# Three denominator terms for four in a masked attention kernel, with one PE step fewer and a finer wait for the mask

## The reference

```python
h = relu(layernorm(x))                       # x: 8 graphs x 1024 nodes x 512, fp32
q, k, v = heads(h @ Wq + bq), heads(h @ Wk + bk), heads(h @ Wv + bv)   # 16 heads of 32
scores = q k^T / sqrt(32);  scores = -inf where adj == 0               # adj: 8 x 1024 x 1024 int32
x + (softmax(scores) @ v) @ Wo + bo
```

## Time and profile before

| | us |
|---|---|
| median of 3 runs | 2085.54 (2085.31 to 2088.58) |
| the profiled execution | 2085.51 |
| its span, first to last instruction | 2083.6 |
| PE busy (matmul) | 1932.5 |
| DVE busy | 1557.3 |
| ACT busy | 1478.1 |
| POOL busy | 1302.1 |

### The profile page before, as it was taken

One profiled execution on the slowest core, in us unless ns is written; L12 is line 12 of the kernel. 1 busy time (PEld: TensorE's weight loads), 2 busy tenths in 40 slices (PEclk: granted clock), 3 DMA queues, 4 the chain that ended last, 5 costly groups with the idle time before them and its releaser, 6 DMA issues.

```text
span 2083.6 us, 40441 instructions
## 1 busy us (share of the span) xinstructions
PE 1932.5 (93%) x14336; PEld 776.5 (37%) x14336; DVE 1557.3 (75%) x1587; ACT 1478.1 (71%) x1765; POOL 1302.1 (62%) x581
## 2 busy tenths in 40 slices
PE   3799899998999999999999999999899998999977
PEld 2334344343344333443334333334333343444312
DVE  5688777878768787687867877778767787767773
ACT  3577786677867788668876778767777677866672
POOL 0377567556666567656667557666557566676574
PEclk8999999999999999999999999999999999999999
DMA  5433244342444324343351434424234332442302
GB/s 177 122 87 96 82 112 132 88 107 64 120 112 124 83 76 132 86 122 86 92 142 56 115 93 117 119 74 119 81 109 122 88 106 66 117 122 64 74 1 81
DMA packets 103222, 206.61 MB, mean 99 GB/s; under 512 B 11616, under 2 KB 11744, under 8 KB 103008
## 3 DMA queue, kind: packets, MB, share of 16 engines
q1 hardware_dynamic: 103008, 203.80, 35.2%
HBM read 153.43 MB, written 50.33 MB: 98 GB/s over the span
## 4 chain that ended last, share of the span: by engine, by line
PE 76%; DVE 7%; issue 6%; DMA 5%; ACT 2%; POOL 1%; SPq 1%; DVEq 0%; ACTq 0%; POOLq 0%
PE ps L694 20%; PE ps L681 19%; PE ps L654 15%; PE ps L705 10%; PE ps L668 7%; PE ps L661 6%; DVE ring L905 4%; DMA k_stack<-k_parts 2%; DMA k_parts<-k_part 1%; SPq L513 1%; DMA edges<-adjT 1%; ACT hT_hi L776 1%; DVE k_part L918 1%; POOL acc L1079 1%; ACT ring L770 1%
## 5 line engine op out<-in xcount | busy, mean ns | idle before, releaser
L905 DVE TENSOR_TENSOR ring<-ps,mask 128x1024 f32<-128x1024 f32 x1024 | 1234.6, 1219 | 435.7 <-PE ps L681 399.9
L770 ACT ACTIVATE ring<-ring 128x1024 f32<-128x1024 f32 x1024 | 1069.7, 1051 | 382.9 <-DVE ring L905 374.6
L1079 POOL TENSOR_TENSOR acc<-ring 128x1024 f32<-128x1024 f32 x256 | 604.1, 2371 | 730.2 <-ACT ring L770 729.4
L681 PE MATMUL ps<-q_stack,k_stack 128*128 128x512 f16 x2048 | 610.4, 382 | 85.2 <-DVE ring L905 61.4
L1079 POOL TENSOR_TENSOR acc<-acc,ring 128x1024 f32<-128x1024 f32 x256 | 617.6, 2432 | 0.0
L694 PE MATMUL ps<-ring,v_sb 128*32 128x512 f32 x4096 | 509.1, 604 | 0.0
L681 PEld LDWEIGHTS ps<-q_stack,k_stack 128*128 128x128 f16 x2048 | 157.1, 98 | 481.8 <-DVE ring L905 246.4
L694 PEld LDWEIGHTS ps<-ring,v_sb 128*32 128x32 f32 x4096 | 100.9, 109 | 252.3 <-issue 218.1
L705 PE MATMUL ps<-acc,ones 128*32 128x512 f32 x1024 | 139.8, 597 | 2.7 <-issue 2.6
L705 PE MATMUL ps<-ring,ones 128*32 128x512 f32 x1024 | 137.3, 592 | 0.0
L661 PE MATMUL ps<-wv_hi,hT_hi 128*128 128x128 f16 x1024 | 103.1, 219 | 3.2 <-DVE k_part L918 3.2
(11 more groups left out here) (80 smaller groups left out, 1593.4 us busy)
## 6 DMA issues: line engine op xcount, KB each, us to landing
x_in<-x SPq DMA_DIRECT2D x168, 256.0 KB, 2.7
edges<-adjT SPq DMA_DIRECT2D x128, 256.0 KB, 2.9
q_stack<-q_parts SPq DMA_DIRECT2D x128, 256.0 KB, 4.9
k_stack<-k_parts SPq DMA_DIRECT2D x128, 256.0 KB, 5.0
q_parts<-q_part SPq DMA_DIRECT2D x32, 512.0 KB, 2.7
k_parts<-k_part SPq DMA_DIRECT2D x32, 512.0 KB, 2.9
out<-x_in SPq DMA_DIRECT2D x56, 256.0 KB, 2.1
ring<-x SPq DMA_DIRECT2D x2, 1024.0 KB, 6.6
```

The lines of the kernel that those rows point to most:

```text
L681: i = nc.tensor.matmul(ps_s(j)[:, hh, :], stack["k"][:, up % 2, h, kt * P:(kt + 1) * P], stack["q"][:, up % 2, h, half * HALF:(half + 1) * ...
L770: nc.scalar.activation(tile, tile, ACT.Exp, scale=SCALE / UP / UP).then_inc(s["prob_ready"], 1)
L905: nc.vector.tensor_tensor(ring[:, slot_of(kt, pair), :].rearrange("p (a n) -> p a n", n=HALF), ps_s(j), mask[:, kt:kt + 1, half * HALF:(ha ...
L1079: nc.gpsimd.tensor_tensor(acc[:, group, pair, :], first_of, ring[:, slot_of(kt, pair), :], ALU.add).then_inc(s["sum_done"], 1)
```

## The change

- A denominator has three terms. A is the sum of key tiles 0 to 3, B of 4 to 6, key tile 7 is read from `ring`. POOL makes 5 x 2 adds a sweep.
- The blocks of a sweep stand in four steps, 6, 10, 14 and 18; those of step 16 move to 18, and A goes from 10 to 14. Step 16 becomes a slot for pieces of chunks.
- DVE's waits for a free slot of `ring` are written anew for this: for the weighted sum of the key tile that was in it, and for the add that read it, or for the last term.
- DVE waits for the mask by key tile, ahead of every second tile, and no longer for eight pieces ahead of a sweep.
- The mask pieces stand behind other tiles of the fourth and the first unit.

```diff
-BLOCKS = {6: ("p0", "p1"), 10: ("p2", "p3", "dA"), 14: ("p4", "p5"), 16: ("p6", "dB", "d6"), 18: ("p7", "d7")}
-TERMS = "AB67"
+BLOCKS = {6: ("p0", "p1"), 10: ("p2", "p3"), 14: ("p4", "p5", "dA"), 18: ("p6", "dB", "p7", "d7")}
+TERMS = "AB7"
+
+SUMMED = {1: 0, 2: 2, 3: 4, 5: 6, 6: 8}
+SUMS = 10
+SUMMED_AT = {"A": 6, "B": 10}
...
-MASK_AT = {3: [17, 18, 20, 22, 24, 26, 28, 30], 0: [1, 3, 5, 7, 8, 9, 11, 13]}
+MASK_AT = {3: [17, 19, 21, 23, 25, 27, 29, 30], 0: [3, 5, 8, 11, 13, 16, 19, 22]}
...
-                    pe.wait_ge(s["sum_done"], 8 * V + 4 * (TERMS.index(term) + 1))
+                    pe.wait_ge(s["sum_done"], SUMS * V + SUMMED_AT[term])
...
-                if kt < RING_KT:
-                    if not very_first:
-                        if kt < 2:
-                            dve.wait_ge(s["pv_done"], 8 * V + kt - 3)
-                            dve.wait_ge(s["sum_done"], 8 * V + 2 * kt - 3 + pair)
-                        else:
-                            dve.wait_ge(s["den_done"], len(TERMS) * V + kt - 3)
-                else:
-                    dve.wait_ge(s["pv_done"], 8 * V + kt - 3)
-                    dve.wait_ge(s["sum_done"], 8 * V + {4: 1, 5: 1, 6: 3, 7: 5}[kt] + pair)
+                before = (V - 1, kt + QT - RING_KT) if kt < RING_KT else (V, kt - RING_KT)
+                if not (kt < RING_KT and very_first):
+                    W, k = before
+                    dve.wait_ge(s["pv_done"], QT * W + k + 1)
+                    if k == QT - 1:
+                        dve.wait_ge(s["den_done"], len(TERMS) * (W + 1))
+                    else:
+                        dve.wait_ge(s["sum_done"], SUMS * W + SUMMED[k if k in SUMMED else k + 1] + pair + 1)
...
-                        if up == 0 and j % SWEEP == 0:
-                            dve.wait_ge(s["mask_ready"], b * 2 * QT + QT * (j // SWEEP + 1))
+                        if up == 0 and j % PAIRS == 0:
+                            dve.wait_ge(s["mask_ready"], b * 2 * QT + j // PAIRS + 1)
...
-                group, k = divmod(kt, 3)
+                group, n = kt // 4, SUMS * V + SUMMED[kt] + pair
                 pool.wait_ge(s["prob_ready"], U * TILES + j + 1)
-                if k == 1 and pair == 0 and not very_first:
+                begins = kt % 4 == 1
+                if begins and pair == 0 and not very_first:
                     pool.wait_ge(s["den_done"], len(TERMS) * (V - 1) + group + 1)
-                if k == 2:
-                    pool.wait_ge(s["sum_done"], 8 * V + 4 * group + pair + 1)
-                first_of = ring[:, slot_of(kt - 1, pair), :] if k == 1 else acc[:, group, pair, :]
+                if not begins:
+                    pool.wait_ge(s["sum_done"], n - 1)
+                first_of = ring[:, slot_of(kt - 1, pair), :] if begins else acc[:, group, pair, :]
...
-                        if j % SWEEP // PAIRS in (1, 2, 4, 5):
+                        if j % SWEEP // PAIRS in SUMMED:
```

## The result

| | before | after |
|---|---|---|
| median of 4 runs, us | 2086.53 (2085.31 to 2088.58) | 2062.02 (2058.85 to 2063.42) |
| ratio, 95% interval | | 0.988 (0.986 to 0.990) |
| the profiled execution, us | 2085.51 | 2058.85, span 2057.1 |
| granted clock over the span | 0.989 | 0.980 |

The change made the kernel 1.2% faster. 2044.1 was forecast, so 18 us of the expected gain are missing, 15 by the profiled execution. The time lies inside the range, near its slow end: the forecast's own bounds ended at 2062, and only rival (b), which did not happen, took the range to 2067. Most of what the forecast says of the sum is in the trace, and the loss is in the one part that it priced at nothing.

What follows compares the result with a forecast made beforehand. TensorE's (PE's) own work was taken as the bound in most of the kernel. The terms -69.1 + 27.0 + 6.0 + 4 - 4.1 - 3.2 - 5.0 + 3 = -41.4 us gave 2044.1 us, range 2021 to 2067.

Steps and rivals of the forecast that it cites:

- rival (b): GpSimd's loop is 1 to 2 us a sweep longer than summed, so sweeps wait: 2064 to 2079 us; chance 0.11.
- Part 1, the term less: In each of 64 sweeps, one denominator block less takes 1.08 us off PE: -69.1 us.
- Part 2, the hole: Two scores-only steps at a unit's end leave PE idle 1.04 us at 26 ends: +27.0 us (15 to 45).
- rival (a): The new idle time at ends of units doesn't appear: 2017 us; chance 0.08.
- Part 3, GpSimd: GpSimd's 128 more adds keep up in every sweep except in the last unit: +6.0 us.
- the loop's 26.4 us: GpSimd's cycle of adds, term B and reciprocal takes 26.4 us, longer than the last sweep's 22.6: +3.8 us there.
- (c): GpSimd's loop sets every sweep, making the kernel slower: 2108 us; chance 0.05.
- Port contention: VectorE's `oT_lo` gets half an add longer beside GpSimd in 24 of 32 cases: +4 us on PE (0 to 12).
- Part 4, mask pieces and the finer wait: Moving mask pieces and waiting by key tile on VectorE costs and gains nothing: 0 us (-3 to +5).
- Part 5: Projection pieces shift as step 16 becomes a slot: -4.1, -3.2, -5.0 and +3 us in the first three units.
- the third unit's k: Its second half starts in the same step in which its bank is freed: +3 us (0 to 6).

Runs made afterwards that it cites:

- p6_step16: The changed kernel with the weighted sum of key tile 6 moved back to step 16, still a slot for chunk pieces; 2054.0 us.
- last_pieces: The changed kernel with mask pieces 2 to 5 of the fourth unit moved back to their old tiles; 2035.1 us.
- mask_before: The changed kernel with all mask pieces and VectorE's coarse mask wait as before the change; 2038.2 us.
- stack_first: The changed kernel with the load of `k_stack` issued one tile earlier in the fourth unit; 2061.0 us.
- store_first: The changed kernel with both the store of `k_parts` and the load of `k_stack` one tile earlier in the fourth unit; 2035.7 us.
- pool_plus: unit3_pieces with one or two more GpSimd adds of 1.28 us in every sweep, results unused; 2047.2 and 2079.3 us.
- unit3_pieces: The changed kernel with the fourth unit's mask pieces at their tiles of before; 2033.3 us.
- mask_alone: The kernel before the change with only the new mask pieces and the new finer wait; 2096.5 us, ratio 1.005.

## Why the prediction was right or wrong

**Part 1, the term less: right.** -69.1 us was forecast on PE, and its own work between the scores fell by 68.2. The extrapolated step of four blocks takes 4.10 us (4.12).

**Part 2, the hole: right.** 1.05 us at each of the 24 ends of units inside the graphs (1.04), and 0.98 in the row of a graph end outside the loop. That is some 27 us, and rival (a) is out. p6_step16 takes the hole away at the cost that its own row shows.

**Part 3, GpSimd: right in the body, short at the end.** Term B follows GpSimd's last add at once in the last three sweeps and in one of the first graph, in no other. There the last sweep was to take the loop's 26.4 us and takes 28.7, from the reciprocal at 1992.29 to that at 2021.00. PE's timeline of after shows it:

```profile
2010.13 1.04 PE L698 MATMUL ps<-ring,v_sb 128*32 128x512 f32 x8
2015.58 1.93 PE L709 MATMUL ps<-acc,ones 128*32 128x512 f32 x8 [4.41 <-POOL acc L1082]
2017.29 1.93 PE L698 MATMUL ps<-ring,v_sb 128*32 128x512 f32 x8
2019.00 1.93 PE L709 MATMUL ps<-ring,ones 128*32 128x512 f32 x8
```

PE waits 4.41 us, and what follows runs at half clock: a block each 1.71 us and not 0.86, three times, 2.6 us that no row could show, since PE did not wait there. So the loop of 26.4 us was right in size, and the term lacked the clock. The output projection starts at half clock too, for 5.1 us (2025.53 to 2030.63), where before it was 2.8. In all, the last unit and what is behind its last scores cost 11.7 us more than before (3.5 lost in the unit, 8.2 behind it), where 6.0 stood in the sum; in last_pieces, mask_before, stack_first and store_first, with the same last unit, it is 9. Rivals (b) and (c) are out as the kernel stands, and the two pool_plus runs confirm how close they are.

**Port contention: too high, from a wrong reading.** `oT_lo` was to cost PE 4 us. Its group in after:

```profile
L962 DVE SCALAR_TENSOR_TENSOR oT_lo<-o_raw,b_up,oT_hi x32: 1274/1364/3350, 136.0 to 2024.2; 128x1024 f16<-128x1024 f32 x32
```

Minimum, median and maximum stand as in the earlier trace rows (1273, 1341, 3482). The mean rose from 1816 to 1843 ns, 0.9 us over all 32. The step that failed is "The median of 1.34 says that most run undisturbed now", and with it that these would get half an add longer. In before, 24 of the 32 already met a GpSimd instruction; in after 31 do. Two of them in after, VectorE's row and the rows of GpSimd beside it:

```profile
990.63 1.34 DVE L962 SCALAR_TENSOR_TENSOR oT_lo<-o_raw,b_up,oT_hi 128x1024 f16<-128x1024 f32 x1
990.84 3.36 POOL L1082 TENSOR_TENSOR acc<-acc,ring 128x1024 f32<-128x1024 f32 x1
...
1052.20 2.37 POOL L1082 TENSOR_TENSOR acc<-acc,ring 128x1024 f32<-128x1024 f32 x1
1052.31 3.35 DVE L962 SCALAR_TENSOR_TENSOR oT_lo<-o_raw,b_up,oT_hi 128x1024 f16<-128x1024 f32 x1
```

Where an add is running, `oT_lo` ends 1.08 us after that add ends; the next add then takes 3.35 us and not 2.37, and ends 2.22 us after `oT_lo`. So each waits for all that is left of the other's instruction. In 15 of the 31 cases of after the running add has 0.25 to 0.37 us left, and in 7 it comes 0.2 us after `oT_lo`, so VectorE pays next to nothing; GpSimd pays the 1.0 us that part 3 has. What the prediction missed is where in an add `oT_lo` falls, which the change hardly moved.

**Part 4, mask pieces and the finer wait: wrong, and this is the miss.** The price was 0 with bounds of -3 and +5, on the ground that "the stores and loads behind them in SP's order have four tiles of slack". The true price is 26 to 29 us (after less store_first and less unit3_pieces). I had looked at what the moved pieces are for, the mask, where the slack is what I said, and VectorE indeed doesn't wait for it. The waits of VectorE that the list of waits puts down to the mask (14.2 us, three times) stand at the jump, where the piece in question was written 15 tiles before; two like them are put down to issue. The last event got the name. But in SyncE's order the store of `k_part` stands behind the load that waits for the piece at tile 21. It is issued 0.3 us after `k_part` is ready in unit3_pieces and 1.77 in after. The "four tiles" are not slack: in before, 11.7 us of them are the way of the store and the load, from the issue at 13.2 us ahead of the scores to the landing at 1.5 us ahead (means of the jumps). From there three things add up: at six ends of graphs the wait itself (0.5 to 1.3 us), and at the five jumps 1.9 us more, as the branch starts late and PE has nothing left to do during it, and the lower clock behind it. So the two parts of the change hit each other: 10 us in the old layout (mask_alone), 29 in the new. That it is the three blocks behind the jump, which the change had just removed, that kept the loss small in the old layout is argued from what is lost behind the jumps (1.1 us there, 6.9 here), and no run put them back alone.

**Part 5: right.** The first unit's wait for `k_part` is gone, the second unit loses nothing any more but the hole, and the third unit's k costs 0.2 us a unit, 1.6 in all where 3 was put.

**What wasn't in the sum.** Without the late `k_stack` the forecast would have been too slow by 11 us (unit3_pieces is at 2033.3). The jumps account for it: in before each loses 2.18 us on the mean ahead of the next graph's second tile and 2.08 in step 0, in unit3_pieces 1.51 and 0.40. That is 2.35 each and 11.7 us over five jumps. The second part is the stall in the middle of step 0's three blocks; after, no blocks stand there. I saw the stall of the earlier trace rows as a cover for the hole, not as something that would shrink. Smaller errors nearly cancel: `oT_lo` and the third unit's k together came out some 5 us better than I put them, the last unit 6 worse. That the measured time lies inside the range is therefore luck in part: a term of 26 to 29 us that was priced at nothing, less these 11, on a range that was wide for another reason.

## What to carry to other kernels

When an instruction that releases a DMA is moved, follow the queue that waits for it, not the data that it makes: list every transfer that stands behind it in that engine's order, and subtract from its slack the time of the whole chain up to its use, store and load included. A term priced at nothing deserves the first experiment, and one that undoes just one list of numbers is cheap. And an idle stretch of a few us on TensorE costs more than its length where the clock falls behind it, so look at what work stands right behind a jump or a wait before taking it away. The same holds for the work ahead of a loop's branch: it hides the jump only if the branch isn't held up by a wait in front of it.

## What the runs showed of the hardware

- **The clock behind idle time.** PE was busy for 1.19 us of the 4 from 1031 to 1035 in after, and the granted clock of the next stretch was 0.50; four matmuls of 512 columns took 1.92 us and not 1.03. With the stall of 0.91 us at the same place in unit3_pieces it didn't fall, nor behind the other four jumps of that kernel, where PE stood for up to 2.08 us.
- **A store takes longer among other transfers.** The same store to `k_parts` took 2.6 to 2.7 us to land at the five jumps of store_first, where no load of edges was issued less than 2 us ahead of it, 3.7 to 4.0 in unit3_pieces, 0.44 us behind such a load, and 4.6 to 6.0 in after, as close behind one and 1.5 us later in the program (5.3 in the rows of stack_first). So 1.5 us of delay at the store became 3.2 at the load. Which transfer it meets when it is late, no run took apart.
- **The jump back of the loop takes PE's sequencer 3.3 to 4.1 us** at 59 of the 70 jumps of all fourteen kernels, with one 16 KB packet of the instruction queue q8 inside it, and 4.1 to 5.2 at the other eleven, with two. Where the loop is left it takes 0.08. PE stood for 0.9 to 2.1 us where it had 14 to 18 matmuls left (unit3_pieces), and for 3.1 to 3.5 where it had one (after).
- **GpSimd's adds don't lengthen the mask adds** (1218 ns with GpSimd 78% busy, 1219 with 62%), but they and `oT_lo`, which has two inputs in SBUF, wait for each other to the end of an instruction: `oT_lo` takes 1274 to 3350 ns, the add behind it 3.35 us and not 2.37. The Trainium skill, GPSIMD Engine Reference, section Specifications, names that contention; the trace agrees.
